# Score matmuls alternated with projection matmuls, and P's two transposes parted by a matmul, in a macaron layer on TensorE

## What is computed

```python
x = x + 0.5 * ffn(layernorm(x), W_base, b_base, W_router, lora_A, lora_B)
x = x + attn(layernorm(x), wq, wk, wv, wo)
x = x + 0.5 * ffn(layernorm(x), W_base, b_base, W_router, lora_A, lora_B)

# attn: 32 query heads, 8 key/value heads, head size 128, rotary positions
q, k, v = rope(x @ wq), rope(x @ wk), x @ wv
allowed = (j <= i) & (j > i - 128)                  # sliding window
attn = softmax(where(allowed, q @ k.T / sqrt(128), lowest))
out = (attn @ v) @ wo

# ffn: base = x @ W_base.T + b_base, and the top 2 of 8 LoRA experts of rank 16
```

## Time and profile before

| | |
|---|---|
| median of 3 runs | 727.85 us (727.74 to 728.06) |
| the profiled execution | 728.14 us |
| its span, first to last instruction | 726.4 us |
| granted clock of TensorE | 1.00 throughout |
| TensorE busy | 714.5 us (98%), 3699 matmuls |
| weight loads busy | 603.5 us (83%) |
| VectorE, ScalarE, GpSimd busy | 522.3, 424.3, 396.5 us |
| iteration of the loop (6 of them) | 76.65 us |

### The profile page before, as it was taken

One profiled execution on the slowest core, in us unless ns is written; L12 is line 12 of the kernel. 1 busy time (PEld: TensorE's weight loads), 2 busy tenths in 40 slices (PEclk: granted clock), 3 DMA queues, 4 the chain that ended last, 5 costly groups with the idle time before them and its releaser, 6 DMA issues.

```text
span 726.4 us, 13750 instructions
## 1 busy us (share of the span) xinstructions
PE 714.5 (98%) x3699; PEld 603.5 (83%) x3699; DVE 522.3 (72%) x1773; ACT 424.3 (58%) x1146; POOL 396.5 (55%) x515
## 2 busy tenths in 40 slices
PE   8999989999999999999999999999999999999998
PEld 6887768888888888888888888888888888887886
DVE  6778776767777777677776677676767776778784
ACT  3456675556664675557655766476657665655440
POOL 2365676535853496447743765368535864374630
PEclk9999999999999999999999999999999999999999
DMA  8140013000310022002100120003000310030002
GB/s 274 56 166 29 0 39 93 15 0 8 100 40 2 0 77 68 1 1 73 58 15 1 58 73 15 1 28 103 15 2 0 102 29 0 1 117 1 0 31 88
DMA packets 25870, 32.34 MB, mean 45 GB/s; under 512 B 5834, under 2 KB 14282, under 8 KB 25300
## 3 DMA queue, kind: packets, MB, share of 16 engines
q1 hardware_dynamic: 25232, 30.69, 13.4%
q10 hardware_dynamic: 580, 1.05, 0.4%
HBM read 27.55 MB, written 4.19 MB: 44 GB/s over the span
## 4 chain that ended last, share of the span: by engine, by line
PE 88%; DVE 4%; POOL 4%; ACT 1%; issue 1%; DMA 1%; SPq 0%; DVEq 0%; POOLq 0%; ACTq 0%
PE bank L1192 33%; PE bank L1253 24%; PE bank L1235 8%; PE bank L1214 7%; PE bank L1153 4%; PE bank L1222 4%; PE bank L1211 2%; POOL wo_lo L405 1%; PE bank L1175 1%; PE bank L1201 1%; PE bank L1212 1%; DVE stats L789 1%; PE bank L1138 1%; PE bank L1126 1%; PE bank L1143 1%
## 5 line engine op out<-in xcount | busy, mean ns | idle before, releaser
L413 POOL TENSOR_TENSOR swap<-swap,rope 128x512 f32<-128x512 f32 x80 | 104.5, 1307 | 116.3 <-ACT swap L593 115.8
L420 POOL TENSOR_SCALAR_AFFINE_SELECT pT_hi_lo<-pT_hi_lo 128x256 fp32r<-128x256 f32 x128 | 52.4, 409 | 140.4 <-DVE pT_hi_lo L943 140.4
L619 ACT ACTIVATE bank<-sm,nmax 128x128 f32<-128x128 f32 x128 | 47.6, 372 | 105.1 <-DVE nmax L928 105.0
L627 ACT ACTIVATE pT_hi_lo<-bank 128x256 fp32r<-128x256 f32 x128 | 49.2, 385 | 95.1 <-PE bank L1222 62.8
L593 ACT ACTIVATE swap<-bank 64x512 f32<-64x512 f32 x160 | 95.1, 594 | 15.0 <-PE bank L1192 12.5
L943 DVE TENSOR_TENSOR pT_hi_lo<-bank,pT_hi_lo 128x256 fp32r<-128x256 f32 x128 | 53.8, 420 | 52.5 <-ACT pT_hi_lo L627 52.2
L430 POOL TENSOR_TENSOR q_lo<-rot,q_hi 128x512 fp32r<-128x512 f32 x64 | 82.7, 1293 | 1.3 <-ACT q_hi L601 1.3
L1253 PE MATMUL bank<-wo_hi,oT_hi 128*128 128x512 f32 x256 | 74.6, 413 | 0.0
L1192 PE MATMUL bank<-xnT_lo,wq_hi 128*128 128x512 f32 x256 | 73.3, 389 | 0.0
L894 DVE TENSOR_TENSOR rot<-bank,rope 128x512 f32<-128x512 f32 x80 | 55.1, 689 | 25.2 <-ACT swap L593 25.1
L1192 PE MATMUL bank<-xnT_hi,wq_hi 128*128 128x512 f32 x256 | 71.9, 393 | 1.0 <-DVE v_lo L914 0.8
(11 more groups left out here) (158 smaller groups left out, 1695.2 us busy)
## 6 DMA issues: line engine op xcount, KB each, us to landing
raw<-in_L_attn_wq SPq DMA_DIRECT2D x32, 256.0 KB, 2.9
raw<-in_L_attn_wo SPq DMA_DIRECT2D x32, 256.0 KB, 2.7
x<-in_L_attn_x SPq DMA_DIRECT2D x4, 512.0 KB, 7.4
raw<-in_L_attn_wk SPq DMA_DIRECT2D x8, 256.0 KB, 2.6
raw<-in_L_attn_wv SPq DMA_DIRECT2D x8, 256.0 KB, 2.6
out<-x SPq DMA_DIRECT2D x8, 256.0 KB, 2.0
raw<-in_L_ffn_W_base ACTq DMA_DIRECT2D x4, 256.0 KB, 5.3
wb_keep_hi<-q_hi SPq DMA_DIRECT2D x1, 1024.0 KB, 4.9
```

The costliest lines, as they stand in the source:

```text
L413: nc.gpsimd.tensor_tensor(w, w, tab, ALU.mult).then_inc(t2_done, 1)
L420: nc.gpsimd.affine_select(pT_both[:, :, 2, h, :], pT_both[:, :, 1, h, :].bitcast(F32), pattern=[[0, 2], [1, P]], compare_op=ALU.is_ge, fil ...
```

## The change

`scores`, `p_transpose`, `values` and `out_project` are cut into steps, so that `group` can place each matmul. A new function says how many of a slot's projection matmuls are held back: four (two in slot 4), and none in the four slots that have no attention tail at the start of group 0 and in the second half of the last group.

```diff
+def between(s, n, plain):
+    return 0 if plain else min(n, 2 if s == 4 else 4)
...
-                        project(target(g, last, hf), 1 if last else 1 - hf, pos[s], pos[s + 1], g if last else g + hf)
+                        held = between(s, pos[s + 1] - pos[s], start or last and hf == 1)
+                        dst = target(g, last, hf), 1 if last else 1 - hf
+                        gw = g if last else g + hf
+                        project(*dst, pos[s], pos[s + 1] - held, gw)
...
-                        if s < SLOTS - 1:
-                            scores(u + 1, s + 1, j, hf)
-                        elif not (last and hf == 1):
-                            scores(u + 1, 0, j + 1, 1 - hf)
-                        if not (start and s == 0):
-                            p_transpose(u - 1, s - 1)
+                        def tail(lo, hi):
+                            if s % G == 1 and not start:
+                                values(beta - 1, prev_hf, (b - 1) % 2, j - (s < G), lo, min(hi, 9))
+                            if s % G >= 2 and not start:
+                                out_project(beta - 1, (b - 1) % 2, s % G - 2, g if b else g - 1, lo, hi)
+
+                        nxt = (u + 1, s + 1, j, hf) if s < SLOTS - 1 else None if last and hf == 1 else (u + 1, 0, j + 1, 1 - hf)
+                        for piece in range(5):
+                            if nxt:
+                                scores(*nxt, piece)
+                            if piece < held:
+                                project(*dst, pos[s + 1] - held + piece, pos[s + 1] - held + piece + 1, gw)
+                        for c in range(2):
+                            if not (start and s == 0):
+                                p_transpose(u - 1, s - 1, c)
+                            if c == 0:
+                                tail(0, 1)
...
-                        if s % G == 1 and not start:
-                            values(beta - 1, prev_hf, (b - 1) % 2, j - (s < G))
-                        if s % G >= 2 and not start:
-                            out_project(beta - 1, (b - 1) % 2, s % G - 2, g if b else g - 1)
+                        tail(1, 12)
```

More of the change, by code:

```diff
@@ L1202, in v_transpose, with scores @@
                 last.then_inc(vt_done, 1)
[L1204 removed]
+            def scores(u, s, j, hf, step_):
                 b, h = s // G, s % G
[L1207 to L1208 removed]
                 q0, q1 = (slice(b * SEQ + i * P, b * SEQ + (i + 1) * P) for i in range(2))
[L1211 to L1213 removed]
+                if step_ == 0:
+                    pe.wait_ge(qlo_done, 5 * j + 2 + h)
+                    wait(pe, norm_done, u - 1)
+                    mm(S[s % 2][:, 0:2 * P], q[0][:, hf, h, q0], k_both[:, :, hf, q0], start=True, stop=False)
+                elif step_ == 1:
+                    mm(S[s % 2][:, 0:P], q[1][:, hf, h, q0], k[0][:, hf, q0], start=False, stop=True)
+                else:
+                    n = step_ - 2
+                    a, c = PASSES[n]
@@ L1214, in scores @@
                     last = mm(S[s % 2][:, 2 * P:4 * P], q[a][:, hf, h, q1], k[c][:, hf, b * SEQ:(b + 1) * SEQ],
                               start=(n == 0), stop=(n == 2))
[L1216 to L1248, removed]
+                    if n == 2:
+                        last.then_inc(s_done, 1)
@@ new lines, in p_transpose, with values @@
+            def p_transpose(u, s, c):
+                if c == 0:
+                    pe.wait_ge(norm_done, u + 1)
+                    wait(pe, ptlo_done, u)
+                last = tp(T[:, c * P:(c + 1) * P], prob[:, s % 2, c * P:(c + 1) * P], ident[:, :])
+                if c == 1:
+                    last.then_inc(t_done, 1)
+            def values(beta, par, b, j, lo=0, hi=9):
+                for step_ in range(lo, hi):
+                    if step_ == 0:
+                        pe.wait_ge(a_free, 6 * j + 6)
+                        pe.wait_ge(ptlo_done, 4 * beta + 4)
+                        wait(pe, otlo_done, 2 * beta)
+                    if step_ == 6:
+                        pe.wait_ge(parted, 4 * beta + 4)
+                    i = 0 if step_ < 3 else 1
+                    blk, kb = ((0, 0), (1, 0), (2, 1))[step_ // 3]
+                    a, c = PASSES[step_ % 3]
+                    last = mm(O[i][:, :], v[a][:, par, 2 * b + kb, :], pT[c][:, blk, :, :],
+                              start=(step_ in (0, 3)), stop=(step_ in (2, 8)))
+                    if step_ in (2, 8):
+                        last.then_inc(pv_done, 1)
@@ new lines, in out_project @@
+            def out_project(beta, par, i, g, lo=0, hi=12):
+                for step_ in range(lo, hi):
+                    a, c = PASSES[step_ // G]
+                    h = step_ % G
+                    if step_ == 0:
+                        pe.wait_ge(conv_hi, wo_pos(g, G - 1) + 1)
+                        pe.wait_ge(othi_done, 2 * beta + i + 1)
+                        if wo_bank(beta, i) is C:
+                            wait(pe, x_added, 2 * beta + i)
+                        else:
+                            pe.wait_ge(otlo_done, 2 * beta + 2)
+                    if h == 0 and c:
@@ L1249, in out_project @@
                         pe.wait_ge(conv_lo, wo_lo(g, G - 1))
-                    if a:
+                    if h == 0 and a:
                         pe.wait_ge(otlo_done, 2 * beta + i + 1)
[L1252 to L1255, removed]
+                    last = mm(wo_bank(beta, i)[:, :], oT[a][:, par, i, h, :], wo_s[c][:, h, :],
+                              start=(step_ == 0), stop=(step_ == 11))
@@ L1257, in group @@
+                    if step_ == 11:
+                        last.then_inc(c_done, 1)
             def group(g, first, last):
@@ L1342, in _ @@
             project(0, 0, 36, 72, 0)
-            scores(0, 0, 0, 0)
+            for piece in range(5):
+                scores(0, 0, 0, 0, piece)
             group(0, True, False)
@@ L1347, in _ @@
             group(KV - 1, False, True)
-            p_transpose(16 * KV - 1, SLOTS - 1)
+            for c in range(2):
+                p_transpose(16 * KV - 1, SLOTS - 1, c)
             lora_router(1, 0)
```

1 line of the change is left out of this document (added).

## The result

The changed kernel takes 733.3 us (median of 4 runs, 733.05 to 733.58) against 727.93 us for the kernel before (4 runs, 727.74 to 728.06): a ratio of 1.0074, 95% interval 1.0057 to 1.0092. It is slower by 5.4 us. I had forecast 728.5, and a range of 724.5 to 731.5; both were wrong. The profiled execution's span is 731.3 us against 726.4.

The account below looks back on a forecast made before the run. The prediction took TensorE's dense matmul stream as the bound. Direct gain 0, neighbours 0 and waits +0.7 us took the profiled 728.14 to 728.8, which stands 0.29 over the median, so 728.5; range 724.5 to 731.5.

Parts of the forecast that it names:

- What bounds: Whole kernel: only TensorE's own stream, busy 76.65 of 76.65 us in a loop iteration, or a new wait in it matters.
- Direct gain of the short ones, 0: 302 short matmuls given long neighbours still cost 0.11 us each; gain taken as 0, bounds 0 and 16.0 us.
- Rival 1: Loads hide behind long matmuls, so a short one costs 0.057 us; 714 us in all, chance 0.15.
- rival 2: Only the 256-wide matmuls in the slots gain, 2.0 us, without the loss beside it; 726.5 us, chance 0.12.
- The figure of some 81 ns for a pair: Cited roofline for a load and matmul of 128 columns; by it 302 pairs would save some 9 us.
- Neighbours: 256-wide matmuls between long ones save 2.0 us, long ones behind short loads start late, up to +3.0; taken as 0.
- My own sign of being wrong: The forecast falls if a slot's seven small matmuls with long neighbours change cost by over 0.013 us.
- Waits, +0.7 us: At five loop turns the scores' earlier wait for prob stalls 0.05 to 0.26 us each, together 0.7 us.
- That wo_lo takes up what the first group loses: First group's block ends up to 0.9 us later, but the following 1.2 us wait for wo_lo covers it: 0.
- Rival 3: At the loop's turn prob comes 0.6 us late five times, 3.1 us in place of 0.7; 730.9 us, chance 0.18.

Follow-up runs that it names:

- e6: Against the kernel before, only the order of a slot's seven small matmuls changed: both transposes right behind the 128-wide score matmul; 723.81 us, ratio 0.9940.
- e7: Against the kernel before, only the order of a slot's small matmuls changed: scores 256, 256, transpose, 256, 256, 128, transpose; 726.39 us, ratio 0.9975.

## Why the prediction was wrong

**What bounds: right.** TensorE's stream is the time, before and after; every run here moved with it.

**Direct gain of the short ones, 0: right.** A short one with long ones on both sides costs 0.11 (337.49 to 337.60), and 0.11 in the quiet series too. Rival 1, the hidden loads, did not come. Of rival 2's 2.0 us there came little: all 512 256-wide ones together cost 0.5 us less than before by the starts of their loads. The figure of some 81 ns for a pair, which I cited from the Trainium skill, "TensorE: Matmul & The Clock Gate", section "Back-to-back issue gap", is not met by these float32 pairs: short ones in a run cost 0.11 each with nothing else going on, and only one directly ahead of a transpose costs less, 0.06.

**Neighbours, "0, between -2.0 and +3.0 us": here it failed.** I priced a late start of the one long matmul behind a short one, at up to 0.01, and let it cancel against cheaper 256-wide ones. In its place the traces show that the disturbance does not end with the next long matmul: up to nine in a row take 0.225 to 0.236, and the whole sequence adds up to 0.048 us over nine steady ones. The change makes five or six groups of small ones in a slot (three in slot 4) instead of one, and moves the place at which the long ones enter their way back. Averages over the loop's slots of each kind, in us, by the starts of all loads; long ones count as what they take over 0.2267 each:

| kernel, block, slots | small ones | long ones among them | long ones behind | sum |
|---|---|---|---|---|
| before, MSMMMTT, 94 | 0.801 | | 0.020 | 0.821 |
| transposes parted, MSMMMTLT, 69 | 0.828 | -0.021 | 0.047 | 0.854 |
| scores alternated, MLSLMLMLMTT, 81 | 0.797 | 0.027 | 0.032 | 0.856 |
| the change, MLSLMLMLMTLT, 69 | 0.821 | 0.011 | 0.040 | 0.873 |
| e6, MSTTMMM, 94 | 0.771 | | 0.014 | 0.785 |
| e7, MMTMMST, 94 | 0.768 | | 0.038 | 0.806 |

So the change costs 0.051 us in such a slot: 0.020 in the long ones behind the block, 0.026 in the four among the scores, and 0.008 where the transposes are parted (there the first costs 0.133 and the long one between them only 0.212), less 0.003 for the 256-wide ones. Over all kinds of slot it is 0.69 us an iteration, 0.043 us a slot, 116 slots: 5.0 us of the 5.4. My own sign of being wrong, over 0.013 us a slot, named this place. The order of before was a lucky one in the kernel: in 71 of the 94 slots its long ones came back after three, at 0.017 in all, where the same order loses 0.054 in the series. By the series alone the change would have lost 0.880 less 0.854, 0.026 us a slot: an estimate of what it costs without that luck.

The row for it was at hand. I took the long steps behind the transposes at 0.227 and counted back from the last one, so what they were over went to the second transpose, as "0.11 or 0.12". A narrower window of the same view has the second long load by itself (356.25 + 0.30 - 0.19 = 356.36):

```profile
356.25 0.30 PEld L1253 LDWEIGHTS bank<-wo_hi,oT_hi 128*128 128x128 f32 x2
```

The transpose thus costs 0.11, the seven 0.80 and not 0.81, and the two long ones up to 356.82 take 0.46 where two steady ones take 0.453.

**Waits, +0.7 us: right in kind, too large.** Two of the five turns hold a load back, by 0.2 us each, and the matmuls come late there by 0.05 and 0.09 (a long matmul covers the rest); the other three don't wait. From prob's end to the load I had counted 0.12 us, and at these two turns it is 0.05. Waits alone cost 0.2 us in the run made for them, which its interval does not tell from none. That wo_lo takes up what the first group loses was right. Rival 3, slower by way of the loop's turn at 730.9, was on the right side for the wrong reason.

**What I read over in the rows.** I put the transposes among the short ones whose cost is the next load. Run e6 shows otherwise: a short one costs its columns, 0.06, when a transpose's load is next (0.03 net of what the matmul ahead of it costs more), and the two transposes keep their 0.11, the second in front of a 256-wide one as before in front of a long one. That a transpose's load takes less is in the earlier trace rows, 0.14 against 0.19 us; that this is the cause is argued from it, not shown, and it can't be all, since a transpose ahead of a transpose costs 0.11 too. The Trainium skill, same page, section "LDWEIGHTS (loading the stationary operand)", gives one time by columns, an estimate of 0.107 us for 128; the 0.11 from a short one's start to its successor's agrees with it, the 0.06 ahead of a transpose does not, and the loads' own rows are longer, 0.19 and 0.14 us.

**Open:** what in TensorE makes the sequence, and what sets the place at which the long ones enter it, so that one order costs 0.821 in the kernel and 0.854 in the series. That totals come in steps of about 0.007 us looks like two parts of it that fall back into step; no run here shows which.

## What to carry to other kernels

In a dense stream of matmuls, look not only at what a small matmul costs but at how many long ones behind it run over their steady time; count such disturbances, and be slow to scatter small matmuls. A float32 matmul of 128 columns directly ahead of a transpose saved 0.03 us here, so that order is worth a try. The order of small ones was worth 0.6% at no cost, and a series behind the kernel's last matmul tries a hundred orders in one run. But it only picks candidates: of the four orders run here it had the dearest right, but one of its two cheapest came third, and it put the blocks that lost 3.4 us each level with or ahead of the kernel before. Each candidate has to be run in the kernel.

## What was not expected of the hardware

After a group of small float32 matmuls, long ones of 512 columns take 0.235, 0.234, 0.235, 0.225, 0.230, 0.236, 0.228, 0.233, 0.232 us and then 0.227 steadily (starts of loads in the series, other engines idle). Every order enters this sequence at its own place, often with one or two long ones off it first: the same seven matmuls with the long ones behind them cost from 0.780 to 0.880 us by their order alone, of which the long ones make 0 to 0.063. A 128-column score matmul costs 0.04 to 0.06 us ahead of a transpose and 0.11 to 0.14 ahead of a 256-wide or long one, but the matmul ahead of it takes back some of that: over the 84 orders the seven small ones are cheaper by 0.03.
